# Attention and mixture-of-experts layer on one core: SyncE's stack loads split around the key store, expert weights loaded in pairs, Pool's bias add in quarters

## What is computed

```python
def attn(x, w_qkv, w_out, b_out):                  # x: (4, 512, 128)
    q, k, v = split(x @ w_qkv.T)                   # 16 heads, 8 wide
    scores = q @ k.T / sqrt(8)                     # only j <= i and i - j < 64
    return (softmax(scores) @ v) @ w_out.T + b_out

def ffn(x, gate_w, gate_b, w1, b1, w2, b2, wg, bg, w3, b3):
    topv, topi = top_k(x @ gate_w + gate_b, 2)
    probs = softmax(topv)
    for e in range(8):
        z = (x @ w1[e] + b1[e]) * (x @ w2[e] + b2[e])
        y = silu(z @ wg[e] + bg[e]) @ w3[e] + b3[e]
        out += sum(probs * (topi == e)) * y
    return out

x = layernorm(x + attn(x)); x = layernorm(x + ffn(x))
```

## Time and profile before

| | before |
|---|---|
| median of 3 runs | 314.18 us (312.11, 314.31, 314.18) |
| the profiled execution | 311.95 us |
| its span, first to last instruction | 310.2 us |
| TensorE busy | 237.9 us, 77% |
| VectorE busy | 217.2 us, 70% |
| ScalarE busy | 154.1 us, 50% |
| Pool busy | 161.0 us, 52% |
| mean granted clock of TensorE | 0.939 of full |
| moved by DMA | 36.50 MB, 118 GB/s over the span |

### The profile page before, as it was taken

One profiled execution on the slowest core, in us unless ns is written; L12 is line 12 of the kernel. 1 busy time (PEld: TensorE's weight loads), 2 busy tenths in 40 slices (PEclk: granted clock), 3 DMA queues, 4 the chain that ended last, 5 costly groups with the idle time before them and its releaser, 6 DMA issues.

```text
span 310.2 us, 7675 instructions
## 1 busy us (share of the span) xinstructions
PE 237.9 (77%) x1791; PEld 174.1 (56%) x1791; DVE 217.2 (70%) x714; ACT 154.1 (50%) x410; POOL 161.0 (52%) x287
## 2 busy tenths in 40 slices
PE   2386579898979998887597878699999999995000
PEld 1155367676757777775355555566766766764000
DVE  6499537888878988886646677677777776774091
ACT  3636537868676968645125633244444334332043
POOL 6654002667666777777643662223464654656151
PEclk9999979999999999999679999999999999999555
DMA  4563425459686979766320112211111111100522
GB/s 119 181 157 91 137 75 143 128 149 273 195 249 189 281 203 268 181 202 240 113 60 3 36 53 68 78 37 51 42 56 32 51 40 45 48 18 7 201 104 101
DMA packets 33988, 36.50 MB, mean 118 GB/s; under 512 B 4972, under 2 KB 30062, under 8 KB 33824
## 3 DMA queue, kind: packets, MB, share of 16 engines
q1 hardware_dynamic: 30864, 29.69, 33.5%
q0 software_dynamic: 2336, 4.37, 4.3%
q10 hardware_dynamic: 752, 2.03, 2.0%
HBM read 25.48 MB, written 11.05 MB: 118 GB/s over the span
## 4 chain that ended last, share of the span: by engine, by line
PE 47%; DVE 14%; SPq 12%; issue 12%; DMA 8%; POOL 3%; ACT 2%; DVEq 0%; ACTq 0%; POOLq 0%
PE bank L1578 9%; PE bank L1550 8%; PE bank L1541 6%; SPq L409 5%; PE bank L1393 3%; DMA k_stack<-k_scratch 3%; PE bank L1573 2%; PE bank L1397 2%; PE bank L1566 2%; PE bank L1412 2%; DMA expert_out<-probs,tile_x 2%; DVE top L954 2%; SPq L422 2%; DVE shift L964 2%; DMA w_up<-expert_out 2%
## 5 line engine op out<-in xcount | busy, mean ns | idle before, releaser
L713 POOL DMA_INDIRECT expert_out<-probs,tile_x x39 | 40.3, 1034 | 58.2 <-DVE probs L1272 56.2
L813 ACT ACTIVATE probs<-bank 128x512 f32<-128x512 f32 x64 | 34.8, 592 | 20.0 <-PE bank L1397 19.6
L664 POOL DMA_INDIRECT routed<-rows,place x32 | 33.2, 1037 | 21.4 <-issue 16.5
L1578 PE MATMUL bank<-w_up,x_unit 128*128 x78 | 41.7, 617 | 0.0
L1550 PE MATMUL bank<-w_gate,x_all 128*128 x156 | 40.4, 382 | 0.5 <-DVE v_aug L1263 0.5
L1277 DVE TENSOR_TENSOR w_rows<-bank,b_up 128x512 f32<-128x512 f32 x39 | 26.8, 688 | 18.5 <-PE bank L1578 18.3
L964 DVE TENSOR_TENSOR shift<-top,delta_block 64x256 fp32r<-64x256 f32 x64 | 30.1, 471 | 11.9 <-PE bank L1397 9.5
L1541 PEld LDWEIGHTS bank<-w_down,xT 128*128 128x128 f32 x156 | 20.4, 190 | 31.2 <-issue 31.2
L888 ACT COPY x_unit<-bank 128x128 f32<-128x128 f32 x39 | 10.3, 264 | 55.3 <-PE bank L1558 55.1
L1393 PE MATMUL bank<-q_stack,k_stack 128*128 128x256 f32 x128 | 28.4, 305 | 10.9 <-issue 7.4
L954 DVE TENSOR_REDUCE top<-bank 128x4 f32<-128x384 f32 x64 | 33.5, 549 | 2.0 <-PE bank L1376 1.3
(11 more groups left out here) (177 smaller groups left out, 538.2 us busy)
## 6 DMA issues: line engine op xcount, KB each, us to landing
k_stack<-k_scratch SPq DMA_DIRECT2D x28, 160.0 KB, 3.2
q_stack<-q_scratch SPq DMA_DIRECT2D x62, 64.0 KB, 2.5
tile_x<-routed SPq DMA_DIRECT2D x39, 65.0 KB, 1.8
k_scratch<-k_parts SPq DMA_DIRECT2D x7, 320.0 KB
q_scratch<-q_parts SPq DMA_DIRECT2D x8, 256.0 KB
w_up<-in_L_ffn_w_dram SPq DMA_DIRECT2D x16, 128.0 KB
w_gate<-in_L_ffn_wg_dram SPq DMA_DIRECT2D x8, 256.0 KB
b_up<-in_L_ffn_b_dram SPq DMA_DIRECT2D x2, 1024.0 KB
```

The costliest lines, as they stand in the source:

```text
L664: eng.indirect_dma_start(routed, bass.IndirectOffsetOnAxis(ap=place[i][:, k:k + 1], axis=0), rows[i][:, k, :], None, bounds_check=SPARE + ...
L713: eng.indirect_dma_start(expert_out, bass.IndirectOffsetOnAxis(ap=tile_x[i][:, P:P + 1].bitcast(I32), axis=0), y[i][:, :], None, bounds_ch ...
L813: eng.activation(probs[t[1] % 2][a][:, 512 * h:512 * h + 512], t_bank[h][:, :], ACT.Exp).then_inc(probs_ready, 1)
L1578: eng.matmul(up_bank[:, :], tile_xT[n[1] % 2][:, :], of_expert(w_up, e[0])).then_inc(up_made, 1)
```

## The change

Three edits, with the waits that follow from them.

1. In an even step SyncE first waits for its stack buffer and for `q_out`, issues four of the eight query stacks, then waits for `k_lo` and stores the keys, then issues the other four and the key stacks.
2. The experts' weights are loaded for two experts at once, in even steps of the loop only, behind the key stacks. The waits on `experts_loaded` are adapted.
3. Pool's add of `b_out` waits for `k_lo` of the second unit and goes in four quarters; the residual waits for all four.

```diff
@@ SyncE, even step
+                    if s is None or s >= 2:
+
+                        wait_apart(eng, wait_value, const_ready, t_filled, count(t, 4, 0))
+                    else:
+                        eng.wait_ge(zeros_ready[i], 1)
+                    eng.wait_ge(q_out, ucount(u, 16, 16))
+                    for part in range(4):
+                        stack_queries(eng, i, part).then_inc(stacked[i], 16)
                     if s != -2:
                         wait(eng, k_hi, ucount(u, 1, 1))
                         wait(eng, k_lo, ucount(u, 1, 1))
                         store_keys(eng, i).then_inc(k_out, 16)
-                    if s is None or s >= 2:
-
-                        wait_apart(eng, wait_value, const_ready, t_filled, count(t, 4, 0))
-                    else:
-                        eng.wait_ge(zeros_ready[i], 1)
-                    eng.wait_ge(q_out, ucount(u, 16, 16))
-                    for part in range(8):
+                    for part in range(4, 8):
                         if s != -2 or part < 8 - POOL_PARTS:
                             stack_queries(eng, i, part).then_inc(stacked[i], 16)
@@ SyncE, weights
-                if s is None:
+                if s is None and t[1] % 2 == 0:
 
                     e = t[0] * 4 + (t[1] - 4)
                     for c, w in enumerate((w1, w2)):
-                        eng.dma_start(w_up[:, bass.ds(e, 1), c, :],
-                                      w[bass.ds(e, 1)].rearrange("e h f -> h e f")).then_inc(experts_loaded, 16)
+                        eng.dma_start(w_up[:, bass.ds(e, 2), c, :],
+                                      w[bass.ds(e, 2)].rearrange("e h f -> h e f")).then_inc(experts_loaded, 16)
                     for held, w in ((w_gate, wg), (w_down, w3)):
-                        eng.dma_start(held[:, bass.ds(e, 1), :, :].rearrange("p e c n -> p (e c) n"),
-                                      w[bass.ds(e, 1)].rearrange("e (c p) n -> p (e c) n", p=P)).then_inc(experts_loaded, 16)
+                        eng.dma_start(held[:, bass.ds(e, 2), :, :].rearrange("p e c n -> p (e c) n"),
+                                      w[bass.ds(e, 2)].rearrange("e (c p) n -> p (e c) n", p=P)).then_inc(experts_loaded, 16)
@@ Pool
                     eng.wait_ge(loaded, 16 * 4)
-                    eng.tensor_tensor(x_all[:, :, :], x_all[:, :, :], bo[:, :].unsqueeze(1).to_broadcast([P, STEPS, P]),
-                                      ALU.add).then_inc(xb_ready, 1)
+                    eng.wait_ge(k_lo, 2)
+                    for q in range(4):
+                        held = x_all[:, 4 * q:4 * q + 4, :]
+                        eng.tensor_tensor(held, held, bo[:, :].unsqueeze(1).to_broadcast([P, 4, P]), ALU.add).then_inc(xb_ready, 1)
@@ Pool, VectorE and TensorE, ahead of the tiles
-            eng.wait_ge(experts_loaded, 16 * (4 * E + 4))
+            eng.wait_ge(experts_loaded, 16 * (2 * E + 4))
@@ VectorE, residual
-                    eng.wait_ge(xb_ready, 1)
+                    eng.wait_ge(xb_ready, 4)
```

More of the change, by code:

```diff
@@ L462, in slot @@
                     i = u[1] % 2
-                    if s != -2:
-                        wait(eng, k_hi, ucount(u, 1, 1))
-                        wait(eng, k_lo, ucount(u, 1, 1))
-                        store_keys(eng, i).then_inc(k_out, 16)
                     if s is None or s >= 2:
@@ L473, in slot @@
                     eng.wait_ge(q_out, ucount(u, 16, 16))
-                    for part in range(8):
+                    for part in range(4):
+                        stack_queries(eng, i, part).then_inc(stacked[i], 16)
+                    if s != -2:
+                        wait(eng, k_hi, ucount(u, 1, 1))
+                        wait(eng, k_lo, ucount(u, 1, 1))
+                        store_keys(eng, i).then_inc(k_out, 16)
+                    for part in range(4, 8):
                         if s != -2 or part < 8 - POOL_PARTS:
```

## The result

The changed kernel takes 314.18 us, the median of 21 runs (310.86 to 319.01); the kernel before, in 21 runs beside them, takes 312.81 (306.63 to 316.41). The ratio is 1.0134, with a 95% interval of 1.0098 to 1.0170. That ratio takes only runs within 1.5% of a kernel's fastest, which keeps 7 of the 21 runs of before and 15 of the change's; by the medians of all runs the ratio is 1.004. So the change makes the kernel slower by 0.4 to 1.3%, where 306.6 and a gain were forecast: nothing of the 6.5 us was gained. I give both measures wherever they differ.

The account below looks back on a forecast made before the run. In attention TensorE was busy 89.57 of 100.50 us, its starts waiting for stacks fed by SyncE's queue. Gains 5.4 + 0.5 + 2.6 - 2.0 = 6.5 us from a base of 313.1 gave 306.6, range 301.5 to 313.

Parts of the forecast that it names:

- Step 1: First unit: early stacks and Pool's held add move TensorE's first start from 40.61 to 35.2, 5.4 us gained.
- The clock's 0.5: Behind TensorE's first start: a wait of about 3 us may keep the clock up, worth 0 to 1.5 us, taken as 0.5.
- Step 2: Second and third waits for stacks in attention, 1.19 and 1.37 us, both vanish: 2.6 us gained.
- Step 3: Four units behind weight bursts: the query store waits for the whole burst; 62.2 us instead of 60.2, loss 2.0.
- store seen: Units behind a burst: query store seen 4.1 us after the next start, then 4.9 us after each landing.
- stalls: SyncE's issuing in the four units: 1 us more for issue stalls, now on the path.
- the stacks' chain: From query store seen to key stacks landed: 2.5 + 0.4 + 2.5 + 2.0 + 3.2 = 10.6 us per unit.
- cases 1: The forecast itself: burst holds the query store, periods near 15.5, gain 4 to 9, 304 to 309 us; chance 0.45.
- case 3: Longer periods eat the gain: at 234 GB/s four units take 67.8 us, net gain 0.9, 310 to 315; chance 0.19.
- case 4: Slower: SyncE's issuing is held too, four units take 72.8 us, net 4.1 slower, 317 us; chance 0.09.
- Case 2: Burst does not hold the query store; later waits of 1.71 and 0.62 vanish too, gain 10.8, about 302; chance 0.27.

Follow-up runs that it names:

- second execution: The changed kernel with no edit, profiled again: this execution took 312.98 us with a span of 311.2; median 314.58 us, ratio 1.0109.
- first execution: The changed kernel's first profiled execution, its slowest: 319.01 us with a span of 317.2.
- the pairs in odd steps: The changed kernel with its two-expert weight loads in odd steps, behind the query store: 305.24 us, ratio 0.9778; on another chip 307.57 us, ratio 0.9841.
- edit 1 alone: The kernel before with only the query stacks split around the key store: 308.72 us, ratio 1.0098, by all runs 0.987.
- the kernel with `w_up` alone: The changed kernel with only `w_up` pairs in the loop's even steps, `w_gate` and `w_down` of all experts in step 12: one run, 304.61 us.
- edit 2 alone: The kernel before with only the weights loaded in pairs in even steps: 316.48 us, ratio 1.0115.

## Why the prediction was wrong

**Step 1, right.** `k_parts` of the second unit was forecast at 25 us, the first start at 35.2. VectorE's and Pool's timelines after:

```profile
24.38 0.49 DVE L1017 TENSOR_TENSOR k_parts<-bank,k_parts 128x320 fp32r<-128x320 f32 x1 [0.43 <-ACT k_parts L795]
...
25.91 2.11 DVE L968 TENSOR_TENSOR shift<-top,delta_block 64x256 fp32r<-64x256 f32 x2
...
29.18 1.96 DVE L968 TENSOR_TENSOR shift<-top,delta_block 64x256 fp32r<-64x256 f32 x2
```

```profile
25.03 5.37 POOL L682 TENSOR_TENSOR x_all<-x_all,bo 128x512 f32<-128x512 f32 x4 [3.13 <-DVE k_parts L1017]
```

The first starts are 35.85 and 34.74. Beside the quarters the `shift` pairs take 2.11 and 1.96 us instead of 0.87, so each holds VectorE 1.1 to 1.2 us as priced, and it is hidden as argued: the next query store goes out at 33.70, behind the key stacks, and no start waits on it.

**The clock's 0.5, not there.** The wait of 2.77 us in the earlier trace rows had left the clock at 1.00, and I took that for the wait of 3 us at the first start. In the second execution the stretches of 5 us behind the first start and behind the start at 82.09 are:

```profile
34.74:39.74 5.00, 5.00 (x36) 4.12 (x37) 2.00 (x6) 2.09 (x5) 0.00 (x0) 0.68 0.34 102
...
82.09:87.09 5.00, 5.00 (x36) 3.97 (x36) 2.17 (x6) 2.11 (x6) 2.72 (x4) 0.66 0.95 276
```

So the clock was down to its lower level for a part of them, after 2.37 and 2.02 us of idle time. The shorter wait at the first start kept its drop (0.66 in the first execution; before, it was 0.69 over the same 5 us). And of the new waits of the later units all but those of 1.06 and 1.19 us brought one with them: 0.66 behind 115.71 and 132.62, and 0.66, 0.70 and 0.52 behind 84.19, 102.48 and 138.16 in the first execution. At 0.66 a stretch of 5 us does 1.7 us less work. The sum had no term for this.

Inside the four units these drops are the 3.0 and 3.3 us of longer TensorE work, but they don't add to the loss: there the next start hangs on SyncE's queue, which from 84 to 125 us waits only for the query store and, for 0.9 to 2.7 us in all, for scatters, never for TensorE's work. At full clock TensorE would have waited longer by as much. Behind the last start the drop does count: it is more than enough for the 1.0 and 1.4 us that the rest of the program takes longer (311.2 - 132.62 = 178.6 and 317.2 - 138.16 = 179.0, against 177.6). So it does where the stacks are there in time: of the pairs in odd steps, the clock is 0.50 over the 5 us behind 81.38, and the next start is 16.8 us later with no wait before it.

**Step 2, right but for the clock.** No waits at 50.79 and 65.76 (49.66 and 64.64 in the second execution). The lead at the third start is 6.6 and 7.7 us, 8.5 forecast with the clock's 0.5. Of it, 1.9 was won behind the first start, where 3.1 was forecast. With edit 1 alone and with the pairs in odd steps the clock stayed at 1.00 behind the first start, and from the first start to the third took 28.5 us instead of 29.9: the missing part is the clock's.

**Step 3, right in mechanism, wrong in size: this is the step that failed.** Its four units were store seen behind the start, 4.1 + 3 x 4.9 = 18.8; from the first stack to the next start, 4 x 10.6 = 42.4; and 1.0 of stalls: 62.2. The same terms, read at the query stacks' first issues:

```
                    forecast   second execution          first execution
store seen            18.8     5.8+5.4+5.1+4.8 = 21.1    5.7+6.8+5.7+6.2 = 24.4
first stack to start  42.4+1.0 11.7+11.4+11.7+12.1 = 46.9  12.7+11.5+10.9+12.8 = 48.0
four units            62.2     68.0                      72.4
```

Of the 5.8 us by which the better execution missed, 3.5 are in the stacks' chain and 2.3 in the store. These are the terms that were too small.

*The stacks' chain.* Issuing takes 7.6 us against the planned 7.4. From the end of the last issue to TensorE's start are 4.0, 3.8, 4.1 and 4.5 us, where I used the 3.2 of the earlier trace rows, a median over all units: on the mean 0.9 us longer, four times 3.6. The burst isn't shown to be the cause. Before has such a case too, from the last key stack's issue at 84.25 to the start at 88.57, 4.3 us, and edit 1 alone one of 4.8, both with single experts. The first execution has 3.5, 3.9, 3.3 and 4.4 us, and loses 3.3 us of the chain in issuing instead (32.9 against 29.6).

*The store.* From the first key stack's issue to the first query stack's the sum had 1.0 + 8.1 + 1.0 = 10.1 us; it took 10.8 to 11.4 in the second execution and 11.4 to 13.2 in the first. Three things. I left out Pool's two scatters a step, 0.13 MB together. The rate was lower than the 275 GB/s of the earlier trace rows, with the share at 0.87. The first row below is the stretch with the store's wait in the first execution, the second the rest until it is seen:

```profile
79.00:89.40 10.40, 7.22 (x63) 5.00 (x63) 5.65 (x21) 5.75 (x15) 6.11 (x12) 0.84 0.87 246
89.40:91.00 1.60, 1.60 (x16) 1.60 (x15) 1.54 (x7) 1.60 (x5) 0.19 (x1) 1.00 0.12 39
```

10.40 us at 246 GB/s are 2.56 MB, against 2.23 reckoned (`x_unit`, 0.13 MB, is in it, though it is issued behind the store), and 246 is nearer to the 234 of the earlier trace rows than to the 275 that I took. Then the engines are nearly still, 0.12, for 1.6 us before the stack is issued at 90.95: from moved to seen it was about 1.5, not 1.0, in this one case; behind the others more traffic follows, and it can't be read.

*A second queue.* In the first of the four units it wasn't the store that was waited for last. SyncE stood at L499 for Pool's scatter of the step, between the store at 66.29 and `x_unit` at 70.79 (3.8 us; 3.9 in the second execution). The store itself landed 4.9 us after its issue, 0.3 us ahead of the first stack (5.0 and 0.3 in the second execution), so this wait cost little. The forecast had no such wait. The scatters take 2.3 to 6.6 us to land in the second execution, but up to 6.5 before, so the burst isn't shown to slow them.

**The cases.** What came is the mechanism that I had in cases 1, 3 and 4 alike. By its time, 314.18, the result is case 3 (310 to 315, given 0.19). The second profiled execution, near the median, took 68.0 us for the units, case 3's 67.8, but not by its terms: case 3 had all of it in the rate, and much of what was measured is in the stacks' chain. The first execution's 72.4 us are case 4's 72.8, given 0.09. I had two rows for the rate, and took 275 GB/s for the forecast and 234 for a rival; at 234 the sum gave a net gain of 0.9 us, and the measured 246 is nearer to that. Two rows with one rate each give no reason to put the faster one into a sum whose every term then lies on the critical path. Without the clock's 0.5, and with the 1.0 to 1.4 us that the rest of the program takes longer, those 0.9 us are no gain.

**Case 2** was wrong on its own terms: without any burst the units still take 60.28 us, so its 10.8 us would have been at most 9 (126.02, 125.71 and 126.83 at the last start, against 132.61, are 6.6, 6.9 and 5.8; only the kernel with `w_up` alone reached 123.73, 8.9).

**What stays open.** The two executions differ by 4.4 us in the four units, in how long the store and the stacks take and in the clock behind each wait; no run shows what decides it. Nor was it tried whether the late landing of the key stacks comes from the weights issued right behind them or from Pool's transfers, nor whether a store in a queue of its own passes a burst that is already under way in SyncE's.

## What to carry to other kernels

Ask of a burst not only whether the engines have room for it on average, but which small store stands behind it in its queue, and who reads that store next: here the burst's place, ahead of the store or behind it, was worth 9 us on one chip; on another the better place was 3 us faster than before. Split a burst so that each piece passes in the slack of one step; in another queue it still held the store that was issued behind it. Price a wait for the clock that it may take down as well as for its own length where the next stage hangs on TensorE's own work, and not where it hangs on a queue; and take "work without the wait" from a run that has no wait, not from a subtraction.

## What the runs showed of the hardware

- TensorE's clock fell after waits of 1.70, 2.02, 2.37, 2.69 and 3.01 us (0.66 to 0.68 over the 5 us behind) and stayed at 1.00 after others of 2.05 and 2.78 us (edit 2 alone, starts 72.66 and 89.91), of 2.77 and, with the pairs in odd steps, of 1.70 (start 129.51). The length of the wait alone does not tell which it will be.
- A DRAM store of 0.26 MB lands 2.1 to 2.2 us after its issue with no weights in the loop, 4.9 to 6.9 us after it behind 1.31 MB of weights in the same queue (eight cases), and 2.2 to 2.9 us with the same weights right behind it (eight cases, both executions of the pairs in odd steps: 2.2, 2.9, 2.2, 2.2 and 2.2, 2.4, 2.2, 2.2).
- A key store of 0.33 MB is followed by its readers after 6.4 and 6.8 us where the same weights had begun to go out 0.7 and 1.4 us before it in another engine's queue, in two cases.
- Six kernels with DMA shares from 0.54 to 0.83 take 60.2 to 60.6 us for the same four units: in these, transfers up to that mean share cost the units nothing. Edits 1 and 3 with one expert a step, 64.07 us at 0.74 in its slowest run, is an exception.
